# Cross-attention and a routed feed-forward part: x comes transposed from memory, its mean is spread by TensorE, and the first batch runs its softmax by halves

## The chip, the cores and the metric

One core of a Trainium2 chip. The metric is device microseconds (us) of one execution. The profiled execution has times of its own, from the hardware profiler.

## The reference

Eight batches (b) of 224 queries and 750 context rows, width 2048, all float32. A layer norm of x, attention of the normalised rows on the context (which is key and value), a residual, a second layer norm, and then a dense layer with sixteen low-rank experts, the top two per row.

```python
def xattn(query, key):
    a = jnp.einsum('bqd,bkd->bqk', query, key)
    e = jax.nn.softmax(a, axis=-1)
    return jnp.einsum('bqk,bkd->bqd', e, key)

x = x + xattn(layernorm(x), ctx)
n = layernorm(x)
base = n @ base_w.T + base_b
hidden, logits = n @ A.T, n @ router_w.T
combine = top-2 of softmax(logits), renormalised
out = x + base + 0.5 * sum over e of combine[e] * (hidden @ B[e].T)
```

## The kernel before

Every product is made of three matmuls of a faster type: an operand is split into a high part (ScalarE copies it into that type) and a low part (VectorE subtracts the high part from the operand), and TensorE adds high x high, high x low and low x high. So in front of each product stands a chain of two engines.

**Batches.** `one(b, stage)` exists on each engine: once for batch 0 ("first"), in a loop for batches 1 to 6 ("mid"), and once for batch 7 ("last"); then come the dense layer and the experts, GT = 56 tiles, which the change leaves as they are. Within a batch TensorE goes through:

- *Scores* (`scores_of`, L753 to L755): the width is 16 blocks k of 128, taken as 8 pairs j. For each pair and each half q of the queries (112 rows each) 2 x 6 matmuls. The context comes transposed from memory (`ctxT`), with four slots in SBUF, but only HR = 2 slots for its high part. So pair j goes ScalarE `ctx_high` (L995, waits until TensorE has done pair j - 2), VectorE `ctx_low` (L1216), TensorE. Each engine has an order written by hand, in which other work is put between the pairs.
- *The batch before* rides along: VectorE takes the statistics of its result x2 (`stats`, L1230), aggregates (L1234), GpSimd raises the variance to -1/2 (L1648), VectorE makes the shift (L1243), ScalarE normalises (L1008, queued between the high parts of pairs 3, 4 and 5), TensorE transposes it (`x2T_of`, L790: 8 transposes of 112x128 a group, 4 groups, ahead of pairs 5, 6, 7 and behind the last), and makes the hidden rows and router logits (L806 to L808). GpSimd adds high and low part of the transposed rows into `xT_st` to be stored.
- *Softmax*: VectorE row maximum (L1248), ScalarE exponentials (L1022), TensorE transposes them (L833).
- *Values* (`outputs_of`, L856 to L858): 24 tiles e (four column chunks c of six row tiles t), six matmuls each. `value_high` (L1017) may run four tiles ahead (NR = 4), `value_low` (L1226) follows it. After a chunk VectorE adds the residual (`residual`, L1261).
- *The next batch's x*: `xn` is loaded (L542), VectorE takes its statistics (half of them in the softmax, half at tiles 4 and 5), ScalarE normalises it at tiles 9 and 10 (L1008), TensorE transposes it in four groups ahead of tiles 13, 14, 16 and 17 (L790), and ScalarE and VectorE split it into `nT_h` and `nT_l` (L989, L1212). x is loaded a second time, into `x2`, for the residual (L549).

The transposes pass through two PSUM slots (`work`), numbered over all stages by `JOBS`: `filled` counts those that TensorE has written, `drained` those that VectorE has read. All loads are issued by SyncE's queue in one written order (`one` under `block.sync`), each behind its waits.

## Time and profile before

| | |
|---|---|
| Median of 3 runs | 1377.2 us (1376.44 to 1383.87) |
| Profiled execution: its own time | 1379.78 us |
| Profiled execution: span from first to last instruction | 1378.0 us |
| TensorE busy | 1344.8 us, 98% |
| VectorE, ScalarE, GpSimd busy | 68%, 45%, 22% |
| Mean granted clock of TensorE | 0.995 of full speed |
| HBM traffic over the span | 261 GB/s |

Busy means that an instruction of the engine was under way; TensorE's matmuls overlap, so their start-to-start distance, not their length, is what one costs. The chain that ended last follows the work back from the end, so its rows tell which engine set the time at each moment.

### The profile page before, as it was taken

Reading aid. Unit: us, or ns where it says so; the run is one execution under the profiler, and the core shown is the slowest. Engines: PE = TensorE matmul, PEld = TensorE weight load, DVE = VectorE, ACT = ScalarE, POOL = GpSimd, SP = SyncE. Lnnn points to the kernel's source line nnn. Section 1 sums busy time; section 2 is a strip of 40 time slices with the busy share of each in tenths; the row PEclk is TensorE's granted clock in tenths of the full one; section 3 lists DMA queues with packets and bytes.
Section 4 is the critical chain, followed back from the end, with each engine's and each line's share of the span. In section 5 each row is a group of like instructions: output and inputs, shape, how many; then the busy total and the mean of one; then the engine's idle time right before and its main releaser. Section 6 shows DMA issues by size and latency. Waiting matters only on the chain.

```text
span 1378.0 us, 17969 instructions
## 1 busy us (share of the span) xinstructions
PE 1344.8 (98%) x6777; PEld 1103.3 (80%) x6777; DVE 936.5 (68%) x1193; ACT 625.3 (45%) x777; POOL 306.4 (22%) x233
## 2 busy tenths in 40 slices
PE   5999999999999999999999999999999999999998
PEld 4778888887878888787888877888788888888887
DVE  6567778778777878868557366787787664464644
ACT  3355655545555554555411356777776211111110
POOL 2001102020200202020614732444453111111110
PEclk9999999999999999999999999999999999999999
DMA  8967768787877868869666678999995978879785
GB/s 297 296 202 256 238 234 249 238 278 242 261 217 257 259 217 262 262 211 234 224 182 170 211 218 271 313 325 318 323 293 149 341 240 260 263 252 284 239 276 160
DMA packets 160248, 345.34 MB, mean 251 GB/s; under 512 B 51680, under 2 KB 68064, under 8 KB 145760
## 3 DMA queue, kind: packets, MB, share of 16 engines
q1 hardware_dynamic: 141600, 277.06, 64.9%
q0 software_dynamic: 10528, 52.85, 12.2%
q10 hardware_dynamic: 8064, 14.68, 3.0%
q8 instruction: 35, 0.57, 0.2%
q14 instruction: 21, 0.17, 0.0%
HBM read 260.87 MB, written 99.41 MB: 261 GB/s over the span
## 4 chain that ended last, share of the span: by engine, by line
PE 82%; DMA 7%; DVE 5%; POOL 3%; issue 2%; ACT 1%; SPq 0%; ACTq 0%; DVEq 0%; POOLq 0%
PE scores L887 11%; PE scores L889 11%; PE scores L888 11%; PE scores L753 6%; PE scores L755 6%; PE scores L754 6%; PE scores L856 6%; PE scores L858 6%; PE scores L857 6%; PE work L790 3%; PE work L923 2%; PE work L924 2%; DMA y_scratch<-y_out,yrow_i 2%; POOL hs_scratch L1706 2%; DMA x<-in_x_dram 2%
## 5 line engine op out<-in xcount | busy, mean ns | idle before, releaser
L887 PE MATMUL scores<-w_h,a_h 128*128 128x512 f32 x896 | 352.0, 393 | 3.3 <-DVE w_l L1464 3.3
L889 PE MATMUL scores<-w_h,a_l 128*128 128x512 f32 x896 | 351.0, 392 | 0.0
L888 PE MATMUL scores<-w_l,a_h 128*128 128x512 f32 x896 | 350.3, 391 | 0.0
L1091 ACT ACTIVATE a_h<-a_in 128x512 fp32r<-128x512 f32 x148 | 83.6, 622 | 315.2 <-DMA a_in<-xT_scratch 205.3
L887 PEld LDWEIGHTS scores<-w_h,a_h 128*128 128x128 f32 x896 | 168.3, 188 | 40.9 <-DVE w_l L1464 4.1
L889 PEld LDWEIGHTS scores<-w_h,a_l 128*128 128x128 f32 x896 | 168.3, 188 | 37.8
L888 PEld LDWEIGHTS scores<-w_l,a_h 128*128 128x128 f32 x896 | 168.4, 188 | 37.0
L1473 DVE TENSOR_TENSOR a_l<-a_in,a_h 128x512 fp32r<-128x512 f32 x148 | 107.5, 774 | 122.2 <-ACT a_h L1091 118.6
L1226 DVE TENSOR_TENSOR raw_l<-raw_in,val_h 128x512 fp32r<-128x512 f32 x192 | 155.6, 827 | 49.1 <-ACT val_h L1017 48.3
L753 PE MATMUL scores<-ctxT_h,nT_h 128*112 128x494 f32 (+1 forms) x512 | 173.4, 339 | 1.1 <-DVE nT_l L1212 1.1
L755 PE MATMUL scores<-ctxT_h,nT_l 128*112 128x494 f32 (+1 forms) x512 | 171.1, 334 | 0.0
L754 PE MATMUL scores<-ctxT_l,nT_h 128*112 128x494 f32 (+1 forms) x512 | 170.9, 334 | 0.0
L1017 ACT ACTIVATE val_h<-raw_in 128x512 fp32r<-128x512 f32 x192 | 118.9, 626 | 107.7 <-PE scores L858 107.7
L856 PE MATMUL scores<-val_h,eT_h 128*112 128x512 f32 (+1 forms) x384 | 156.9, 409 | 5.9 <-DVE raw_l L1226 4.0
L1216 DVE TENSOR_TENSOR ctxT_l<-ctxT_in,ctxT_h 128x1500 fp32r<-128x1500 f32 x64 | 109.4, 1719 | 70.4 <-ACT ctxT_h L995 69.5
L858 PE MATMUL scores<-val_h,eT_l 128*112 128x512 f32 (+1 forms) x384 | 152.9, 398 | 0.0
L857 PE MATMUL scores<-raw_l,eT_h 128*112 128x512 f32 (+1 forms) x384 | 152.6, 397 | 0.0
L995 ACT ACTIVATE ctxT_h<-ctxT_in 128x1500 fp32r<-128x1500 f32 x64 | 92.4, 1454 | 121.5 <-PE scores L755 110.5
L1531 DVE TENSOR_TENSOR b_hl<-b_in,b_hl 64x2048 fp32r<-64x2048 f32 x43 | 99.6, 2319 | 42.4 <-ACT b_hl L1107 39.4
L1673 POOL TENSOR_TENSOR res<-res,bias_b 128x512 f32<-128x512 f32 x42 | 63.6, 1516 | 290.1 <-DMA res<-x_scratch 265.9
L1648 POOL TENSOR_TENSOR rs<-ve,mhalf 112x2 f32<-112x2 f32 x16 | 15.4, 964 | 420.4 <-DVE ve L1238 420.4
L1664 POOL TENSOR_TENSOR xT_st<-nT_h,nT_l 128x896 f32<-128x896 f32 x32 | 72.4, 2267 | 157.7 <-DVE nT_l L1212 157.7
(150 smaller groups left out, 1981.9 us busy)
## 6 DMA issues: line engine op xcount, KB each, us to landing
ctxT_in<-in_ctxT_dram SPq DMA_DIRECT2D x64, 750.0 KB, 7.6
raw_in<-in_ctx_dram SPq DMA_DIRECT2D x32, 1280.0 KB
a_in<-xT_scratch SPq DMA_DIRECT2D x37, 1024.0 KB
w_in<-in_wT_dram SPq DMA_DIRECT2D x32, 512.0 KB, 10.4
x<-in_x_dram SPq DMA_DIRECT2D x8, 1792.0 KB, 10.4
y_add<-y_scratch SPq DMA_DIRECT2D x56, 256.0 KB, 7.0
late_y<-y_scratch SPq DMA_DIRECT2D x56, 256.0 KB, 6.2
xn<-in_x_dram SPq DMA_DIRECT2D x7, 1792.0 KB, 15.4
```

What stands on the lines that cost most here:

```text
L753: pe.matmul(out, qh, ch, start=(k == 0), stop=False)
L754: pe.matmul(out, qh, cl, start=False, stop=False)
L755: last = pe.matmul(out, ql, ch, start=False, stop=(k == KD - 1))
L856: pe.matmul(out, eh, vh, start=(t == 0), stop=False)
L857: pe.matmul(out, eh, vl, start=False, stop=False)
L858: last = pe.matmul(out, el, vh, start=False, stop=(t == NT - 1))
L887: pe.matmul(o, ah, wh, start=(k == 0), stop=False)
L888: pe.matmul(o, ah, wl, start=False, stop=False)
L889: last = pe.matmul(o, al, wh, start=False, stop=(k == KD - 1))
L1017: act.activation(val_h[0:rows, e % NR, :], raw_in[0:rows, c, t, :], ACT.Copy).then_inc(val_high, 1)
L1216: dve.tensor_tensor(ctxT_l[:, j % LR, :, :], ctxT_in[:, j % LR, :, :], as_f32(ctxT_h[j % HR][:, :, :]), ALU.subtract).then_inc(ctx_ready, 1)
L1226: dve.tensor_tensor(raw[0:rows, c, t, :], raw_in[0:rows, c, t, :], as_f32(val_h[0:rows, e % NR, :]), ALU.subtract).then_inc(val_ready, 1)
```

## The change

x is handed over in a second layout, `xT`: for each batch 128 partitions x 16 blocks x 224 queries. The kernel loads that in place of transposing, into `xT_in`, which lies on the same bytes as `nT_l`. The rows of x are then loaded once per batch, into one of two buffers in turn (`rows`), and serve for the statistics and for the residual. Of the layer norm only the mean is taken off ahead of the scores: TensorE transposes a broadcast of the mean (`spread_mean`, ahead of tile 10), which gives a row of means on all partitions, and VectorE subtracts it in four parts (`centre`, at tiles 14 and 17 and at pairs 2 and 4 of the next batch). The factor 1/sigma goes into the exponentials, as their scale, and into the row maximum, by one more small multiplication. High and low parts of x stand at tiles 16, 17, 19, 20 and at pairs 3 and 5. VectorE's statistics of the next x stand at tiles 4 to 7, those of the old batch at pairs 0 and 2 (five and three), and the shift is moved behind pair 3's `ctx_low`. The next load of rows stands where the second load of x stood; in batch 7 the first four weights are loaded there too, later than before.

Batch 0 still normalises and transposes its own rows; for its residual x is loaded again. It takes pairs 6 and 7 together, first for half 0 of the queries and then for half 1, with the transposes of half 0's exponentials between the two pairs of half 1, and the first four value tiles for half 0, then for half 1. The loops over batches 1 to 6 are written out.

```diff
-LN1_AT = (9, 10)
-QT_AT = (13, 14, 16, 17)
+STATS_AT = (4, 5, 6, 7)
+MEAN_AT = 8
+SPREAD_AT = 10
+CENTRE_AT = (14, 17)
+X_HIGH_AT = (16, 19)
+X_LOW_AT = (17, 20)
...
-            nT_l = sb("nT_l", [P, KD, LQ], F32R, first)
+            nT_l, xT_in = sb_in("nT", [P, KD, LQ], first)
...
+        rows = [xn, x2]
+        mean_b = bias_b[:, 0, 0:LQ]
...
+            def load_row(b):
+                sp.dma_start(rows[b % 2][:, :, :], x_v[b]).then_inc(row_loaded[b % 2], 16)
+            def load_xT(b):
+                sp.dma_start(xT_in[:, :, :], xT[b]).then_inc(xT_loaded, 16)
...
                 if not last:
                     if first:
+                        load_row(1)
                         sp.wait_ge(filled, job_no("pre", 0, "qT", NX - 1) + 1)
-                    else:
-                        sp.wait_ge(filled, job_no("mid", b, "x2T", 0))
-                    sp.dma_start(xn[:, :, :], x_v[b + 1]).then_inc(xn_loaded, 16)
+                        sp.dma_start(xn[:, :, :], x_v[0]).then_inc(xres_loaded, 16)
                     for j in range(LR - 1):
                         score_done(sp, b, NPC - LR + j)
                         load_ctxT(b + 1, j)
                 if not first:
                     sp.wait_ge(filled, job_no(stage, b, "x2T", NX - 1) + 1)
-                sp.dma_start(x2[:, :, :], x_v[b]).then_inc(xres_loaded, 16)
                 if not last:
+                    if not first:
+                        load_row(b + 1)
                     score_done(sp, b, NPC - 1)
                     load_ctxT(b + 1, LR - 1)
+                    if not first:
+                        sp.wait_ge(filled, job_no(stage, b, "hid") + 1)
+                        sp.wait_ge(xT_staged, b * NX)
+                    load_xT(b + 1)
                     raw_again(b, 0)
...
+                if stage == "first":
+                    pe.wait_ge(ctx_ready, b * NPC + NPC)
+                    pe.wait_ge(drained, job_no("pre", 0, "qT", NX - 1) + 1)
+                    for q in range(NQ):
+                        for k in range(KD - 2 * CP, KD - CP):
+                            last = products(k, q)
+                        if q == NQ - 1:
+                            last.then_inc(score_step, 1)
+                            exps_T(stage, b, 0)
+                        for k in range(KD - CP, KD):
+                            last = products(k, q)
+                        last.then_inc(scores_done, 1)
+                    return
...
+            def spread_mean(stage, b):
+                pe.wait_ge(aggr1, (b + 2) * NQ)
+                for q in range(NQ):
+                    take(job_no(stage, b, "mB", q))
+                    pe.transpose(place(stage, "mB", q)[:, 0:QT], mv1[:, q, 0:1].to_broadcast([QT, P]),
+                                 ident[0:QT, 0:QT]).then_inc(filled, 1)
...
+                if stage == "first":
+                    pe.wait_ge(drained, job_no(stage, b, "eT", 0) + 1)
+                    for e in range(NR):
+                        if e == NR - 1:
+                            exps_T(stage, b, 1)
+                        pe.wait_ge(val_ready, b * (CH * NT) + e + 1)
+                        value_products(b, e, 0)
                 pe.wait_ge(drained, job_no(stage, b, "eT", NQ - 1) + 1)
+                if stage == "first":
+                    for e in range(NR):
+                        value_products(b, e, 1).then_inc(val_used, 1)
...
-                    if stage != "last" and e in QT_AT:
-                        pe.wait_ge(ln1_done, b * NQ + NQ)
-                        transpose_rows(stage, b, "qT", xn, QT_AT.index(e))
+                    if stage != "last" and e == SPREAD_AT:
+                        spread_mean(stage, b)
...
-            with pe.Fori(1, NB - 1) as b:
+            for b in range(1, NB - 1):
...
+            def x_high_part(b, n):
+                act.wait_ge(centred, (b - 1) * NX + n + 1)
+                act.activation(four_blocks(nT_h, n), four_blocks(xT_in, n), ACT.Copy).then_inc(x_high, 1)
             def one(b, stage):
                 for j in range(HR, NPC):
                     ctx_high(b, j)
+                    if stage != "first" and j in (3, 5):
+                        x_high_part(b, 2 + (j - 3) // 2)
...
+            def centre(b, n):
+                if n == 0:
+                    dve.wait_ge(xT_loaded, b * 16)
+                    dve.wait_ge(filled, job_no(stage_of(b - 1), b - 1, "mB", NQ - 1) + 1)
+                    dve.tensor_copy(mean_b.rearrange("a (q p) -> a q p", q=NQ),
+                                    work[:, :, 0:QT]).then_inc(drained, NQ)
+                    dve.wait_ge(drained, job_no(stage_of(b - 1), b - 1, "mB", NQ - 1) + 1)
+                cut = slice(4 * n, 4 * n + 4)
+                dve.tensor_tensor(xT_in[:, cut, :], xT_in[:, cut, :],
+                                  mean_b.unsqueeze(1).to_broadcast([P, 4, LQ]), ALU.subtract).then_inc(centred, 1)
...
+                dve.reduce_max(nraw[:, q:q + 1], all_scores(q), AX.X, negate=True).then_inc(max_step, 1)
+                dve.wait_ge(rstd1, b + 1)
+                dve.wait_ge(max_step, (b - 1) * NQ + q + 1)
+                dve.tensor_tensor(nmax[:, q:q + 1], nraw[:, q:q + 1], rs1[:, q:q + 1],
+                                  ALU.mult).then_inc(max_ready, 1)
...
                 for j in range(NPC):
+                    if j >= HR:
+                        ctx_low(b, j)
                     if old and j == 3:
                         shift(mv2, rs2, nb2, rstd2, bias2, b - 1)
-                    if j >= HR:
-                        ctx_low(b, j)
-                    if old and j < 2:
-                        if j == 0:
-                            dve.wait_ge(x2_done, b * (NQ * CH))
-                        for i in range(4 * j, 4 * j + 4):
-                            stats(x2, st2, stat2, i)
+                    if old and j == 0:
+                        dve.wait_ge(x2_done, b * (NQ * CH))
+                        for i in range(5):
+                            stats(rows[(b - 1) % 2], st2, stat2, i)
                     if old and j == 2:
+                        for i in (5, 6, 7):
+                            stats(rows[(b - 1) % 2], st2, stat2, i)
+                        dve.wait_ge(stat2, b * (NQ * CH))
                         aggregate(st2, mv2, aggr2)
                         variance(mv2, ve2, aggr2, var2, b - 1)
+                    if old and j in (2, 4):
+                        centre(b, 2 + (j - 2) // 2)
+                    if old and j in (3, 5):
+                        x_low_part(b, 2 + (j - 3) // 2)
...
+                    if new and e in STATS_AT:
+                        n = STATS_AT.index(e)
+                        if n == 0:
+                            dve.wait_ge(row_loaded[(b + 1) % 2], (b + 2) // 2 * 16)
+                        for i in range(2 * n, 2 * n + 2):
+                            stats(rows[(b + 1) % 2], st1, stat1, i)
```

## Rows read from the trace of the kernel before

**Rows 1.** The page, section 1: busy us of each engine and share.
```profile
PE 1344.8 (98%) x6777; PEld 1103.3 (80%) x6777; DVE 936.5 (68%) x1193; ACT 625.3 (45%) x777; POOL 306.4 (22%) x233
```

**Rows 2.** The chain that ended last, by time: start us, us, what.
```profile
50.08 24.61 DMA x<-in_x_dram
...
163.34 0.77 PE work L790 x8
...
242.62 0.77 PE work L790 x8
...
725.42 1.11 DVE hg L1289
```

**Rows 3.** Timeline of TensorE, values of batches 1 and 2.
```profile
163.18 0.93 PE L790 MATMUL work<-ident,xn 112*128 112x112 f32 x8
163.88 0.47 PE L856 MATMUL scores<-val_h,eT_h 128*112 128x512 f32 x1
...
226.96 0.30 PE L822 MATMUL work<-ident,hT 80*112 80x80 f32 x2
```

**Rows 4.** The page, section 6: DMA issues, KB, us to landing.
```profile
x<-in_x_dram SPq DMA_DIRECT2D x8, 1792.0 KB, 10.4
```

**Rows 5.** Timeline of TensorE, scores of batch 2.
```profile
181.55 0.39 PE L753 MATMUL scores<-ctxT_h,nT_h 128*112 128x494 f32 x1
...
189.69 0.28 PE L755 MATMUL scores<-ctxT_h,nT_l 128*112 128x256 f32 x1
189.94 0.47 PE L753 MATMUL scores<-ctxT_h,nT_h 128*112 128x494 f32 x1
```

**Rows 6.** Timeline of VectorE, start of batch 2.
```profile
183.19 4.85 DVE L1230 BATCH_NORM_STATS2 st<-x 112x6 f32<-112x512 f32 x8
188.16 1.72 DVE L1216 TENSOR_TENSOR ctxT_l<-ctxT_in,ctxT_h 128x1500 fp32r<-128x1500 f32 x1
189.80 0.38 DVE L1234 BATCH_NORM_AGGREGATE mv<-st 112x2 f32<-112x24 f32 x2
```

**Rows 7.** Timeline of ScalarE, start of batch 2.
```profile
185.97 1.46 ACT L995 ACTIVATE ctxT_h<-ctxT_in 128x1500 fp32r<-128x1500 f32 x1 [6.46 <-PE scores L755]
...
191.38 2.10 ACT L1008 ACTIVATE x<-x,nb,rs 112x2048 f32<-112x2048 f32 x1
```

**Rows 8.** Groups by shape: busy us, mean ns.
```profile
L1212 DVE TENSOR_TENSOR nT_l<-work,nT_h 128x896 fp32r<-128x896 f32 x64 | 69.4, 1086 | 15.3 <-ACT nT_h L989 15.2
```

**Rows 9.** Timeline of GpSimd: the power operation beside VectorE.
```profile
68.80 1.66 POOL L1648 TENSOR_TENSOR rs<-ve,mhalf 112x2 f32<-112x2 f32 x1 [49.55 <-DVE ve L1238]
...
190.46 0.69 POOL L1648 TENSOR_TENSOR rs<-ve,mhalf 112x2 f32<-112x2 f32 x1 [36.81 <-DVE ve L1238]
...
231.82 1.10 POOL L1648 TENSOR_TENSOR rs<-ve,mhalf 112x2 f32<-112x2 f32 x1 [9.58 <-DVE ve L1238]
```

**Rows 10.** Timeline of VectorE, beside the last of these.
```profile
231.67 1.29 DVE L1226 TENSOR_TENSOR raw_l<-raw_in,val_h 128x512 fp32r<-128x512 f32 x2
```

**Rows 11.** Timeline of TensorE: its idle times, in square brackets.
```profile
55.86 0.79 PE L833 MATMUL work<-ident,prob 112*128 112x112 f32 x6 [1.27 <-ACT prob L1022]
58.37 0.49 PE L856 MATMUL scores<-val_h,eT_h 128*112 128x512 f32 x1 [1.71 <-DVE eT_l L1212]
...
76.78 0.77 PE L856 MATMUL scores<-val_h,eT_h 128*112 128x512 f32 x1 [2.68 <-DVE raw_l L1226]
...
994.37 0.50 PE L923 MATMUL work<-b_hl,s_hh 128*128 128x512 f32 x1 [1.19 <-DVE y_out L1539]
```

**Rows 12.** Stretches: busy us by engine, granted clock, DMA share, GB/s.
```profile
70.00:75.00 5.00, 4.10 (x18) 2.79 (x16) 1.13 (x4) 4.31 (x3) 0.46 (x1) 1.00 0.99 301
76.00:84.00 8.00, 7.22 (x20) 5.23 (x21) 4.29 (x8) 2.11 (x4) 0.00 (x0) 0.57 0.27 78
994.00:999.00 5.00, 4.63 (x20) 3.85 (x21) 3.48 (x4) 3.36 (x4) 3.25 (x2) 1.00 0.77 276
```

**Rows 13.** Timeline of VectorE, batch 0, the low part of pair 7.
```profile
47.08 1.72 DVE L1216 TENSOR_TENSOR ctxT_l<-ctxT_in,ctxT_h 128x1500 fp32r<-128x1500 f32 x1 [1.20 <-ACT ctxT_h L995]
```

More of the change, by code:

```diff
@@ L162, in xattn_ffn_kernel @@
         "pre": group("qT", NX),
-        "first": group("eT", NQ) + group("qT", NX),
-        "mid": BEFORE + group("eT", NQ) + OLD + group("qT", NX),
+        "first": group("eT", NQ) + group("mB", NQ),
+        "mid": BEFORE + group("eT", NQ) + OLD + group("mB", NQ),
         "last": BEFORE + group("eT", NQ) + OLD,
@@ L189, in act_no, with side_of, stage_of @@
         return number(stage, b, (name, n), BY_ACT)
+    def side_of(b, c):
+        return (c + 1) % 2 if b > 0 else c % 2
+    def stage_of(b):
+        return "first" if b == 0 else "mid"
     def slot_of(stage, name, n=0):
@@ L756, in products @@
                     return last
-                for j in range(NPC - 1):
+                for j in range(NPC - 1 if stage != "first" else NPC - 2):
                     if stage != "first" and j in X2T_BEFORE:
-                        x2T_of(stage, b, b - 1, x2, (X2T_BEFORE.index(j),))
+                        x2T_of(stage, b, b - 1, rows[(b - 1) % 2], (X2T_BEFORE.index(j),))
                     if stage == "first" and j in (1, 2):
@@ L837, in outputs_of, with exps_T @@
-            def outputs_of(stage, b):
+            def exps_T(stage, b, q):
+                pe.wait_ge(exp_done, b * NQ + q + 1)
+                take(job_no(stage, b, "eT", q))
+                slot = slot_of(stage, "eT", q)
+                for t in range(NT):
+                    at = (t // 3) * BANK + (t % 3) * QT
+                    last = pe.transpose(work[:, slot, at:at + QT],
+                                        prob[:, q, t * P:(t + 1) * P], ident[0:QT, 0:QT])
+                last.then_inc(filled, 1)
@@ L863, in one @@
                 if stage != "first":
-                    x2T_of(stage, b, b - 1, x2, (NX - 1,))
+                    x2T_of(stage, b, b - 1, rows[(b - 1) % 2], (NX - 1,))
                     hidden_of(stage, b, 0, HID_EARLY)
-                exps_T(stage, b)
+                if stage != "first":
+                    for q in range(NQ):
+                        exps_T(stage, b, q)
                 if stage != "first":
@@ L1047, in one @@
                     high(stage, b, "x2T", NX - 1, four_blocks(nT_h, NX - 1), 2, 2 * LQ)
+                three = lambda q: eT_h[:, q, :, :].rearrange("p (k i) c -> p k (i c)", k=2)
+                if stage == "first":
+                    high(stage, b, "eT", 0, three(0), 2, 3 * QT)
                 exponentials(b, 1)
-                for q in range(NQ):
-                    high(stage, b, "eT", q, eT_h[:, q, :, :].rearrange("p (k i) c -> p k (i c)", k=2), 2, 3 * QT)
+                for q in range(1 if stage == "first" else 0, NQ):
+                    high(stage, b, "eT", q, three(q), 2, 3 * QT)
                 for e in range(NR, CH * NT):
@@ L1121, in _ @@
             one(0, "first")
-            with act.Fori(1, NB - 1) as b:
+            for b in range(1, NB - 1):
                 one(b, "mid")
@@ L1410, in one, with exps_low @@
                         value_low(b, 2 * (j - (NPC - 2)) + 1)
+                def exps_low(q):
+                    three = lambda tile: tile[:, q, :, :].rearrange("p (k i) c -> p k (i c)", k=2)
+                    low(stage, b, "eT", q, three(eT_h), three(eT_l), 2, 3 * QT)
                 row_max(b, 0)
@@ L1416, in one @@
                     x2T_low(NX - 1)
-                if new and old:
-                    dve.wait_ge(xn_loaded, b * 16 + 16)
-                    for i in range(4):
-                        stats(xn, st1, stat1, i)
-                for q in range(NQ):
-                    three = lambda tile: tile[:, q, :, :].rearrange("p (k i) c -> p k (i c)", k=2)
-                    low(stage, b, "eT", q, three(eT_h), three(eT_l), 2, 3 * QT)
+                for q in range(0 if old else 1, NQ):
+                    exps_low(q)
                 if old:
@@ L1446, in one @@
                         tile_low(0, (FIRST_A_AT.index(e),))
-                    if new and e - 3 in QT_AT:
-                        n = QT_AT.index(e - 3)
-                        low(stage, b, "qT", n, four_blocks(nT_h, n), four_blocks(nT_l, n), 2, 2 * LQ)
                     if c >= 1 and t == 3:
@@ L1562, in _ @@
             one(0, "first")
-            with dve.Fori(1, NB - 1) as b:
+            for b in range(1, NB - 1):
                 one(b, "mid")
```

133 lines of the change are left out of this document (68 added, 65 removed).

## The prediction

> **What bounds the kernel now.** I read the page first: TensorE is busy for 98% of the span, VectorE 68%, ScalarE 45% [rows 1]. Then the chain in order of time. It returns to the same transposes every 79.28 us (163.34 to 242.62) and names almost nothing but TensorE between batch 1 and batch 6, so in the attention part a microsecond taken off TensorE is a microsecond of the program, as long as nobody makes it wait. Batch 0 is the exception: the chain there has a DMA of 24.61 us, the second load of x [rows 2]. The routed part behind batch 7 is not touched; I carry it over whole. Last I laid the timelines of TensorE, VectorE and ScalarE side by side for batch 2, where the change puts new work.
>
> The sum is made against the profiled execution: span 1378.0 us, its own time 1379.78 us. The median of the runs is 1377.2, so 2.6 below that execution; I carry every difference over to the median. A difference under 0.5% (6.9 us) can't be told from none by a measurement of this kernel.
>
> **Transposes of x out of the value stage.** One group of eight starts at 163.18 and the next value product at 163.88; the chain gives the group 0.77 us [rows 2, 3], restart included. Four groups in each of batches 0 to 6: 28 x 0.77 = -21.6 us. Added are two transposes of the mean per batch. The pair of the hidden part takes 0.30 with its tail [rows 3]; the new ones are as wide as those of x (0.77/8 = 0.10 each), so 2 x 0.10 and about 0.07 of restart = 0.26, times 7 = +1.8 us. ScalarE loses the two normalisations per batch; it is off the path there, worth nothing.
>
> **VectorE in the value stage.** Per batch the eight statistics now all stand at value tiles 4 to 7 (four stood in the softmax before), and a copy of the mean, two subtractions of it and two low parts stand at 14 to 20. A value tile is 6 x 0.231 = 1.39 us on TensorE. Tiles 4 to 10 ask VectorE for 7 low parts of 0.61, 8 statistics of 0.6, 0.8 for mean and variance, 0.45 for the hidden copy and 1.6 for the first residual: 11.9 us against 9.7 of TensorE, with about 2.3 us of lead at the start. It just fits, with 0.3 us left at tile 10. Tiles 14 to 21 ask 12.3 against 11.1, with about 3 of lead: fits. I take 0. The bound is the row load: it is issued where the load of x was, behind the last transposes of the old batch, and that one took 10.4 us to land [rows 4]; tile 4's statistics come 9 us after the issue (the hidden transposes ahead of tile 2 are at 226.96 [rows 3]). A load that is 1.4 late eats the lead and costs 0.9 per batch, 5.4 us. Against it: the load of xn that stood ahead of it in the queue is gone, 1.8 MB less backlog. The transposed x is issued at the start of the values and is wanted 16 us later: hidden.
>
> **VectorE and ScalarE in the score stage: the new wait.** Here the order of the hand-offs is what counts. A pair of context blocks j needs TensorE's j-2 done, then ScalarE's high part (1.46), then VectorE's low part (1.72), and TensorE spends 4.13 on a pair ((189.81-181.55)/2 [rows 5]). That leaves 0.6 us of slack a pair. Batch 2 by the new order: five statistics from 183.19 at 0.6 end at 186.2; the high part of pair 2 ends at 185.97+1.46 = 187.43; its low part starts there (before, it stood behind eight statistics until 188.16 and ended at 189.88, and TensorE, free at 189.81, began at 189.94 with a restart of 0.08: 0.2 gained) [rows 5, 6, 7]. Then VectorE issues at 189.10 three statistics (1.8), aggregation (0.4), variance (0.1) and the subtraction of the mean. The latter has no row; the low part of the same 896 elements takes 1.09 [rows 8], an operation of that size with a broadcast operand 1.11 [rows 2]. I take 1.05, bounds 0.5 and 1.6. So pair 3's low part starts at 192.6 and ends at 194.3; TensorE wants it at 189.81+4.13 = 193.9: it stops for 0.4, and 0.08 of restart. The shift, which before ran ahead of that low part, is now behind it: 194.2+0.16 = 194.4. ScalarE's first normalisation of the old batch waits for the shift, holds ScalarE for 2.0 and is queued ahead of the high part of pair 4: 196.4 + 1.46 = 197.9, low part to 199.6. TensorE wants pair 4 at 194.4+4.13 = 198.5: it stops for 1.1 and 0.08 more. Pair 5 has the old batch's transposes ahead of it and is on time. Net of the 0.2 gained: +1.5 us in each of batches 1 to 7, +10.5 us. Bounds: with the subtraction at 0.5 it is +0.9 a batch, at 1.6 it is +2.5; and a reason to be all wrong would be that the old order has slack I don't see, 0.
>
> The small power operation on GpSimd stands between variance and shift. It takes 0.69 when VectorE is idle and 1.10 when two low parts run beside it, once 1.66 [rows 9]; the low parts beside the 1.10 still took 1.29 for two, their usual 0.61 apiece and a tail [rows 10]. So I take it done by 193.2, before the shift is due, at no cost; if it is held until pair 3's low part is through (as the 1.66 was), the shift moves 0.7 back, +4.9 us over seven batches. The Trainium skill's page "SBUF — State Buffer", section "SBUF: two separate sides", says that a VectorE operation with two SBUF inputs and a GpSimd operation that reads SBUF exclude each other for a whole instruction, the loser fully blocked. By that rule GpSimd's 0.69 would also be added to pair 3's low part, +0.7 a batch, or about 5 us in all; the row of 1.29 for two low parts beside it doesn't show it.
>
> The extra product of the row maximum with 1/sigma (0.2 us, twice) delays the exponentials; the transposes that wait for them had about 1.4 us to spare. And the low parts of the exponentials lose the four statistics ahead of them, 0.1 gained. I take -0.1 a batch, -0.6 us.
>
> **Batch 0.** Before: softmax and the second load of x leave TensorE idle for 1.27, 1.71 and 2.68 us [rows 11], and after the last the clock is at its lower level for a while: 0.57 of full speed from 76 to 84 [rows 12], 0.43 x 8 = 3.4 us, some 0.5 of it on idle time, so 2.9 lost. The batch ends a period before 181.55, at 102.3. In the new queue the load of x stands right behind the row of batch 1 and no longer behind three contexts; the 2.68 and its clock are gone. What comes instead: TensorE now waits for pairs 6 and 7 before it starts pair 6. It would start at 45.6 (the high part of pair 7 waits for the same event, 47.08-1.46), but pair 7's low part ends at 48.80 [rows 13]: 3.2 us idle, and the clock falls after such a gap [rows 11, 12], 2 more. The halves then hide most of the softmax (0.5 is left); the exponentials of the second half leave 1.1; and the four tiles done by halves take VectorE's lead away in front of its statistics (2). Last, the transposed x of batch 1: x and all ahead of it landed at 50.08+24.61 = 74.7 with a full queue [rows 2, 12]; behind it come 0.75 and 1.8 MB at 301 GB/s, so it lands near 83. VectorE asks for it at tile 14, from about 80, and then owes the copy, two subtractions, a low part, the residual and the low parts of tiles 15 to 18, 7.6 us in all: tile 18 starts at 90.6, and six tiles of 1.39 end at 98.9. That is 3.4 us ahead, of which 3.1-0.3 = 2.8 are the transposes and the mean already counted: -0.6 beside the terms above. Bounds: 0 to 8 us ahead.
>
> **Loops written out, instructions fetched once each.** Batches 0 and 7 are written out already, under a full DMA queue, and TensorE's waits there have data behind them. 0. Weights 0 to 3 load 16 us later in batch 7 and are wanted at tile 15: hidden. HBM traffic is the same.
>
> **Sum.** -21.6 +1.8 +10.5 -0.6 -0.6 = -10.5. Median 1377.2-10.5 = 1366.7 us (0.8% faster), a mid batch 77.9 instead of 79.3. Its own range, with batch 0 and the subtraction at their nearer values, 1361 to 1371.
>
> **Rivals.**
> 1. The score stage has no new wait. For it: only 0.4 and 1.1 us. Against: each hand-off has its row. 1366.7-10.5 = 1356.
> 2. The score wait is a step bigger, by GpSimd's late power operation or a row load that lands late: +5, so 1371.6, within 0.5%. For it: 1.66 in one row; 10.4 us of landing.
> 3. Slower: the score-stage wait lets the clock fall in every batch. The place is pair 4; the price by the row of batch 0 is 2.9 us, seven times 20.3, so 1387. It decides where a gap grows past the 1.19 at 994 (full clock after it) toward 2.68 (clock fell) [rows 11, 12]. My gap is 1.1, with 0.4 four microseconds ahead of it.
> 4. Nothing changes: VectorE, with 4 us more work a batch, gives the 3 us back in the values as well. 1376.
>
> **Chances.** Forecast 0.48, rival 1 0.14, rival 2 0.20, rival 3 0.08, rival 4 0.10. Faster by over 0.5%: most of the forecast (0.42), rival 1, a fourth of rival 2: 0.61. Slower: 0.08. Same: 0.31. Range: from rival 1 to rival 4, 1355 to 1377.
>
> **What would show it.** The transposes of x fall from 512 to 288 and the mean's 14 appear. TensorE's idle time ahead of the first score product of pairs 3 and 4, released by the low part of the context, is 0.4 and 1.1 us in batches 1 to 7 (10 us in all, 1.1 before). ScalarE's normalisation starts near 12.9 us after the batch's first score, not 9.8. In batch 0 a gap of 3 us ends at 48.9 and no wait for x. I am wrong if the period of a mid batch is 76.3 (rival 1) or 79 (rival 4), if the granted clock falls in mid batches (rival 3), or if batch 0 ends later than 102.

## The result and the profile after

The changed kernel takes 1375.0 us (median of 14 runs, 1372.1 to 1376.7); the kernel before, timed beside it, 1381.0 us (14 runs, 1373.6 to 1386.2). The ratio is 0.9959, 95% interval 0.9942 to 0.9976: 0.41% or 6 us faster, under the 0.5% that the prediction set as its bound, and 8 us over its 1366.7. The profiled execution has a span of 1373.0 us.

The page's first section after the change (busy us, share of the span, instructions), beside [rows 1]:

```profile
PE 1330.2 (97%) x6567; PEld 1083.7 (79%) x6567; DVE 968.8 (71%) x1235; ACT 599.2 (44%) x763; POOL 325.4 (24%) x233
```

VectorE has 32 us more to do, TensorE 15 us less. I laid the start of every batch and stage of both timelines beside each other (us). A batch and its score stage begin with the first score product; the value stage goes from the first value product to the next batch:

| | before | after | forecast of the difference |
|---|---|---|---|
| start of batch 1 | 102.23 | 98.69 | -3.4, measured -3.5 |
| score stage, batches 1 to 7 | 42.3 to 42.6 | 44.6 | +1.4, measured +2.05 |
| value stage, batches 1 to 6 | 36.74 | 33.85; batches 3, 5, 6: 34.56, 34.04, 34.35 | -2.8, measured -2.9 and +0.2 for late rows, on average |
| start of batch 7 | 578.16 | 570.68 | -11.9, measured -7.5 |
| from there to the end | 799.9 | 802.3 | +1.4, measured +2.5 |

The chain of the changed kernel in batch 2 (start, us, what; of the 15 longest pieces between 60 and 240 us these are the batch's) shows where the score stage loses its time:

```profile
181.44 1.47 ACT ctxT_h L1061
182.93 1.72 DVE ctxT_l L1286
184.65 1.80 DVE st L1301 x3
187.14 3.10 POOL rs L1749
190.63 1.84 issue
192.47 1.44 ACT ctxT_h L1061
193.93 1.73 DVE ctxT_l L1286
```

[Rows 2] had almost nothing but TensorE here. Now the chain leaves it for GpSimd's power operation `rs`: 3.10 us, where [rows 9] have 0.69. The same place on the timeline of VectorE:

```profile
186.89 0.17 DVE L1309 TENSOR_SCALAR ve<-mv 112x2 f32<-112x2 f32 x1
186.97 1.09 DVE L1338 TENSOR_TENSOR nT_in<-nT_in,bias_b 128x896 f32<-128x896 f32 x1
187.97 1.71 DVE L1286 TENSOR_TENSOR ctxT_l<-ctxT_in,ctxT_h 128x1500 fp32r<-128x1500 f32 x1
190.26 0.16 DVE L1314 SCALAR_TENSOR_TENSOR nb<-mv,rs 112x2 f32<-112x2 f32 x1 [0.58 <-POOL rs L1749]
```

`ve` frees GpSimd at 187.06. VectorE goes straight on with the subtraction and pair 3's low part, until 189.68. The power operation is under way all that time and ends 0.55 us behind them, and the shift `nb` comes at 190.26. Behind it on ScalarE, in its order:

```profile
190.46 2.10 ACT L1074 ACTIVATE x<-x,nb,rs 112x2048 f32<-112x2048 f32 x1 [1.42 <-DVE nb L1314]
192.47 1.43 ACT L1061 ACTIVATE ctxT_h<-ctxT_in 128x1500 fp32r<-128x1500 f32 x1
```

The old batch's normalisation, then pair 4's high part; VectorE's low part follows at 193.93, and TensorE, which was through with pair 3 at 194.1, waits:

```profile
195.71 0.48 PE L779 MATMUL scores<-ctxT_h,nT_h 128*112 128x494 f32 x1 [1.61 <-DVE ctxT_l L1286]
```

That gap is 1.61 or 1.62 us in each of batches 1 to 7. It does not bring the clock down. The windows behind the gap and over the mid batches (PEclk is the third number from the end):

```profile
195.00:203.00 8.00, 7.29 (x46) 6.35 (x47) 5.76 (x5) 6.89 (x8) 0.00 (x0) 1.00 0.98 339
100.00:660.00 560.00, 546.47 (x3056) 445.92 (x3055) 469.32 (x605) 291.55 (x352) 96.30 (x43) 1.00 0.78 243
```

In batch 0 the forecast gap is there, at its length (3.2 forecast), with a granted clock of 0.60 from 51 to 55 us behind it, and so is the gap of the second half's exponentials:

```profile
50.89 0.75 PE L779 MATMUL scores<-ctxT_h,nT_h 128*112 128x494 f32 x1 [3.30 <-DVE ctxT_l L1286]
...
66.20 0.49 PE L893 MATMUL scores<-val_h,eT_h 128*112 128x512 f32 x1 [1.01 <-DVE eT_l L1282]
```

### The profile page after: what moved, and what is told of

Same layout as the page of the kernel before. It is cut to its first block, busy times and chain, and to the rows that moved or that the text cites. A ratio compares the mean times of both kernels' runs of the same rounds, so it can differ in the third digit from the quotient of the medians.

```text
span 1373.0 us, 16807 instructions
## 1 busy us (share of the span) xinstructions
PE 1330.2 (97%) x6567; PEld 1083.7 (79%) x6567; DVE 968.8 (71%) x1235; ACT 599.2 (44%) x763; POOL 325.4 (24%) x233
## 4 chain that ended last, share of the span: by engine, by line
PE 79%; DVE 5%; DMA 4%; issue 2%; ACT 2%; POOL 1%; ACTq 0%; DVEq 0%; POOLq 0%
PE scores L953 14%; PE scores L955 14%; PE scores L954 14%; PE scores L893 6%; PE scores L895 6%; PE scores L894 6%; PE scores L779 4%; PE scores L781 4%; PE scores L780 4%; DMA y_scratch<-y_out,yrow_i 2%; PE work L989 2%; PE work L990 2%; PE work L840 2%; DVE ctxT_l L1286 2%; ACT ctxT_h L1061 1%
## 5 line engine op out<-in xcount | busy, mean ns | idle before, releaser
L779 PE MATMUL scores<-ctxT_h,nT_h 128*112 128x494 f32 (+1 forms) x512 | 175.8, 343 | 16.2 <-DVE ctxT_l L1286 14.6
L1574 DVE TENSOR_TENSOR a_l<-a_in,a_h 128x512 fp32r<-128x512 f32 x148 | 103.9, 749 | 105.6 <-ACT a_h L1161 101.7
L893 PE MATMUL scores<-val_h,eT_h 128*112 128x512 f32 (+1 forms) x384 | 153.9, 401 | 3.2 <-DVE raw_l L1296 1.4
L1749 POOL TENSOR_TENSOR rs<-ve,mhalf 112x2 f32<-112x2 f32 x16 | 31.5, 1966 | 403.3 <-DVE ve L1309 403.3
L779 PEld LDWEIGHTS scores<-ctxT_h,nT_h 128*112 128x112 f32 x512 | 90.6, 177 | 33.2 <-DVE ctxT_l L1286 18.4
```

Of the source, the lines that this page charges most:

```text
L779: pe.matmul(out, qh, ch, start=(k == 0), stop=False)
L893: pe.matmul(out, eh, vh, start=(t == 0), stop=False)
```

## The experiments

Fourteen runs follow; two of them (e9, e12) are the two kernels unchanged. A time without an interval is one execution, and of such times only the stages are compared: the part from the first score of batch 7 to the end, whose code differs only in that batch, takes between 794.8 and 802.3 us in these profiles.

### What holds the score stage: e1, e2, e6

e1 takes the subtraction out from between variance and low part:

```diff
-                    if old and j in (2, 4):
-                        centre(b, 2 + (j - 2) // 2)
+                    if old and j == 4:
+                        centre(b, 3)
...
+                    if new and e == 22:
+                        centre(b + 1, 2)
```

> The third subtraction of the mean (part 2) is moved from VectorE's pair 2 to value tile 22 of the batch before; all else as in the changed kernel. In the changed kernel pair 3 of a mid batch starts 12.62 us after the batch's first score and pair 4 at 18.60, TensorE idle 1.61 ahead of it, and the power operation on GpSimd lasts 3.10. Theory A (GpSimd is shut out while VectorE's operations with two SBUF inputs follow each other without a break): the power operation lasts 2.0 to 2.4 since only the low part of pair 3 stands beside it, pair 3 at 12.4, pair 4 at 17.7, so 0.9 off a batch and 6 us in all. Theory B (the power operation is slow for another reason, the wait is only the sum of VectorE's own work): it stays at 3.1, and pair 4 moves by less than 0.3 since the shift still waits for it. Theory C (the port costs nothing): 0.7 to 1.1 for the power operation, pair 4 at 17.0.

Measured: 1364.8 us. Pair 4 starts 17.70 after the first score, the score stage is 43.69, 0.9 less in every batch. GpSimd and VectorE in batch 2:

```profile
186.93 2.19 POOL L1751 TENSOR_TENSOR rs<-ve,mhalf 112x2 f32<-112x2 f32 x1 [31.28 <-DVE ve L1309]
```

```profile
186.85 1.72 DVE L1286 TENSOR_TENSOR ctxT_l<-ctxT_in,ctxT_h 128x1500 fp32r<-128x1500 f32 x1
```

The low part ends at 188.57, the power at 189.12: again 0.55 behind. Theory A, to the digit.

e2 leaves the subtraction and puts the shift ahead of the low part:

```diff
+                    if old and j == 3:
+                        shift(mv2, rs2, nb2, rstd2, bias2, b - 1)
                     if j >= HR:
                         ctx_low(b, j)
-                    if old and j == 3:
-                        shift(mv2, rs2, nb2, rstd2, bias2, b - 1)
```

> One part undone: the shift of the old batch stands ahead of pair 3's low part again, all else as in the changed kernel. VectorE then has to wait for GpSimd behind the subtraction of the mean. Theory A: the power operation lasts about 2.1 (shut out during the one subtraction, then 0.7 alone), the shift comes near 11.7 us after the batch's first score, pair 3 starts at 13.5, pair 4 at 17.7 with no idle time ahead of it: 0.9 off a batch. The rival, that the order of shift and low part is worth nothing because it only moves the wait from pair 4 to pair 3: pair 4 stays at 18.3 to 18.6.

Measured: 1363.7 us. Pair 3 at 13.36, pair 4 at 17.57, the score stage 43.46:

```profile
184.48 1.46 POOL L1749 TENSOR_TENSOR rs<-ve,mhalf 112x2 f32<-112x2 f32 x1 [31.25 <-DVE ve L1309]
```

```profile
184.31 1.09 DVE L1338 TENSOR_TENSOR nT_in<-nT_in,bias_b 128x896 f32<-128x896 f32 x1
185.97 0.16 DVE L1314 SCALAR_TENSOR_TENSOR nb<-mv,rs 112x2 f32<-112x2 f32 x1 [0.58 <-POOL rs L1749]
186.05 1.72 DVE L1286 TENSOR_TENSOR ctxT_l<-ctxT_in,ctxT_h 128x1500 fp32r<-128x1500 f32 x1
```

VectorE now stops behind the subtraction, and GpSimd gets in there: the power ends 0.54 behind the subtraction's end at 185.40. Both pairs come as theory A has them, 0.1 earlier still; only the power is shorter than its 2.1. The rival (pair 4 at 18.3 to 18.6) is out.

e6 puts an operation with one input in the power's place:

```diff
-                pool.tensor_tensor(rs[:, :], ve[:, :], mhalf[:, :], ALU.pow).then_inc(sem_rstd, 1)
+                pool.tensor_scalar(rs[:, :], ve[:, :], 1.0, None, ALU.add).then_inc(sem_rstd, 1)
```

> The changed kernel, but GpSimd's power of two inputs (variance and exponent) is an addition of a constant to one input, so 1/sigma is replaced by a wrong value and the output is not the reference's; every order and wait is the same. It asks whether GpSimd is shut out beside VectorE's subtractions because it reads two inputs, or because it reads and writes SBUF at all. Theory A (any GpSimd operation on SBUF is shut out until VectorE's run of two-input operations has ended): the operation lasts 2.9 to 3.1 us in the score stage of every batch as the power does (3.09), pair 4's first score stands 18.6 us after the batch's first. Rival B (one input gets through): it lasts under 1 us, VectorE's shift starts right behind pair 3's low part without the 0.58 of idle time, and pair 4 starts at 18.0 to 18.1, 3.5 us less over seven batches. Rival C: in between, it ends during the low part but the start is delayed by the subtraction.

Measured: 1366.3 us, score stage 44.1, pair 4 at 18.12. GpSimd, and the low part beside it:

```profile
187.72 2.61 POOL L1749 TENSOR_SCALAR rs<-ve 112x2 f32<-112x2 f32 x1 [32.06 <-DVE ve L1309]
```

```profile
188.55 1.71 DVE L1286 TENSOR_TENSOR ctxT_l<-ctxT_in,ctxT_h 128x1500 fp32r<-128x1500 f32 x1
```

It is shut out as well, until VectorE's run ends at 190.26, and is through 0.07 later. So A for the blocking; pair 4 stands where B had it, because an addition needs 0.5 us less than the power once it is let in. What the profile gives as the power's length is two things: waiting for VectorE's run to end, and 0.55 behind it.

### Batch 0: e3, e4

e3 runs batch 0 in the old order (pairs 6 and 7 apart, softmax and values whole).

> The halves of batch 0 undone: scores, softmax and values of batch 0 in the order of the kernel before; transposed x, mean and everything else as in the changed kernel. Theory A (the halves cost more by the double wait at pair 6 and by the lost lead of VectorE at tiles 4 to 10 than they hide of the softmax; it is the earlier load of x that helps): batch 1 starts at 95 to 96.5 instead of 98.7. Rival (the halves are what shortens batch 0): batch 1 starts later than 99, since the softmax leaves 3 us idle again and the clock falls behind it.

Measured: 1368.7 us. TensorE's gaps are the two of before [rows 11]:

```profile
58.33 0.79 PE L870 MATMUL work<-ident,prob 112*128 112x112 f32 x6 [1.27 <-ACT prob L1065]
60.84 0.49 PE L881 MATMUL scores<-val_h,eT_h 128*112 128x512 f32 x1 [1.71 <-DVE eT_l L1257]
```

Batch 0 takes 76.8 us, 2.7 less than in the changed kernel, and batch 1 starts at 96.1: theory A. The first pair of batch 0 takes 4.9 to 7.7 us in these traces, whatever the kernel, so it is better left out: from the second pair on, batch 0 takes 69.7 here and 72.7 in the changed kernel (72.7 in e1, e2 and e6 too, whose batch 0 is the same; 74.0 in e12, where the lower clock lasts longer). So the halves with their double wait cost 3.0 us more than they hide. e4 keeps the halves and splits their wait:

```diff
-                    pe.wait_ge(ctx_ready, b * NPC + NPC)
+                    pe.wait_ge(ctx_ready, b * NPC + NPC - 1)
...
+                        if q == 0:
+                            pe.wait_ge(ctx_ready, b * NPC + NPC)
```

> As the changed kernel, but in batch 0 TensorE waits for the context of pair 6 before pair 6 and for that of pair 7 only before the first product of pair 7. Theory A (the double wait costs its 3.3 us and the clock behind it): the idle time ahead of pair 6 is gone, 1.3 is left in front of pair 7's first product, the clock stays up and the values of batch 0 begin 3 to 4 us earlier (61.5 now), batch 1 starts near 95. Rival (another wait takes its place, VectorE's statistics or the transposed x, which lands at 79.7): batch 1 starts less than 1 us earlier.

Measured: 1371.0 us, batch 0 takes 76.2, 3.3 less, and its values begin at 57.9 instead of 61.5: theory A. What is left of the gap, now ahead of pair 7, left the clock up (the product takes 0.48, not 0.75, and the granted clock is 1.00 from 46 to 60 us):

```profile
50.82 0.48 PE L779 MATMUL scores<-ctxT_h,nT_h 128*112 128x494 f32 x1 [1.26 <-DVE ctxT_l L1288]
...
62.58 0.48 PE L895 MATMUL scores<-val_h,eT_h 128*112 128x512 f32 x1 [1.01 <-DVE eT_l L1284]
```

From the second pair on it takes 69.6 us, no less than the 69.7 of e3 without any halves. So the 3.0 us are the double wait; the halves by themselves bring nothing that one profile of each shows.

### The orders together: e7, e8

e7 is e1, e2 and e4 in one kernel.

> The changed kernel with three orders of the first four experiments together: the shift stands ahead of pair 3's low part, the subtraction for part 2 of x is moved from the score stage to value tile 22 of the batch before, and in batch 0 TensorE waits for pair 6 first and for pair 7 only after it. Theory A (what the change lost is the VectorE queue between variance and shift, and the single wait in batch 0): variance is followed by nothing, the power takes 0.69 to 0.75 us beside an idle VectorE, pair 3 starts 12.6 to 12.8 us and pair 4 16.8 to 17.0 us after the batch's first score with no gap over 0.3, the score stage takes 42.6 to 42.8 (44.59 in the changed kernel, 42.55 before), seven times -1.9 = -13, batch 0 is 3.3 shorter: 16 us under the changed kernel, about 1359 us, 1.6% under the kernel before. Rival B: the subtraction at value tile 22 is in the way of the next batch's first low parts and gives 0.5 to 1 us a batch back: 1362 to 1366. Rival C: the idle 0.7 us on VectorE only moves the gap to pair 3: it starts at 13.3 and the score stage stays at 43.4, about 1364.

Measured: 1357.7 us (6 runs), ratio to before 0.9834, 0.9800 to 0.9868. Pair 3 at 12.59, pair 4 at 16.79, score stage 42.68 in batches 2 to 7, where the kernel before has 42.6 (42.3 in batch 7). Batch 1 takes 43.14, and batch 0 is 2.6 shorter from its second pair on, not 3.3. GpSimd has VectorE out of its way:

```profile
183.83 0.69 POOL L1753 TENSOR_TENSOR rs<-ve,mhalf 112x2 f32<-112x2 f32 x1 [31.28 <-DVE ve L1311]
```

Theory A; what the changed kernel lost in these stages is the place of three steps. Batch 3's value stage is still 34.47 and batch 5's 34.48. e8 moves the statistics for that:

```diff
-STATS_AT = (4, 5, 6, 7)
-MEAN_AT = 8
-SPREAD_AT = 10
+STATS_AT = (6, 7, 8, 9)
+MEAN_AT = 10
+SPREAD_AT = 12
```

> e7 and in addition the statistics of the new batch at value tiles 6 to 9 instead of 4 to 7 (mean and variance at 10, spread of the mean by transposes at 12). Theory A (in batch 3, and at times in batches 1, 5 and 6, VectorE waits at tile 4 for a row load of 10 us): the wait at the statistics is gone, batch 3's value stage falls from 34.8 to 33.85 and all seven are alike, 1 to 2 us less than e7. Rival B: the statistics then collide with the first residual at tile 9 and the lead is gone at tile 10: every value stage is 0.5 us or more longer, 3 us or more slower than e7. Rival C: no difference: the late load of batch 3 is only the last of several waits there.

Measured: 1359.1 us (6 runs), 0.9841, 0.9809 to 0.9872, not to be told from e7. The value stages of batches 1 to 6 are 34.43 to 34.45: the wait is gone, and batches 1 to 6 pay 0.6 for it each, as rival B had it, though not with its 3 us in the whole.

### The written-out loops: e5, e9 to e14

e5 is the kernel before with this edit on TensorE, ScalarE and VectorE:

```diff
-            with pe.Fori(1, NB - 1) as b:
+            for b in range(1, NB - 1):
```

> The kernel before with nothing changed but its three loops over batches 1 to 6 written out, as the change writes them. Theory A (the forecast: instructions fetched once each cost nothing under a full DMA queue): the same time as the kernel before within 0.2%, score stage of a mid batch (first score to first value) 42.6 us and its period 79.3, as before; the instruction queue's packets rise from 35 to about 50. Rival B: part of the small result is the price of the written-out loops: 3 to 6 us slower than the kernel before, with gaps on TensorE that nothing releases. Rival C: a loop turn costs something at its branch, so writing it out alone gains 1 us or more over six batches.

Measured: 1372.2 us (10 runs; before 1382.3), ratio 0.9934, 0.9909 to 0.9959. Theories A and B missed. C's number is met by the mid batches, which gain 0.16 us each (79.17), 1 us in all, but the kernel is faster by more than the whole change. In the two profiles the rest lies where there is no loop: 5.0 us behind the first score of batch 7 and 2.3 us in batch 0, where the second load of x takes 22.7 us in place of 24.6, and the gap of 3.31 ahead of the product that waits for `w_l` (841.14 in the kernel before) is not there.

> The kernel before, unchanged, profiled a second time. In its first profile TensorE had gaps of 2.68 us at 76.78 and 3.31 us at 841.14 that the profile of the same kernel with its loops written out (e5, 0.66% faster) lacks, while its mid batches differ by only 0.16 us each. Theory A (the loops cause the gaps in some lasting way): both gaps are there again, each over 2 us, and the period of a mid batch is 79.3. Theory B (a load in batch 0 and one in the routed part land earlier or later from one execution to the next): at least one of the two is gone or under 1 us, and others may stand elsewhere; the period is 79.3 all the same.

Measured: 1378.8 us; period 79.3, batch 0's gap 1.80 in place of 2.68, so that neither theory is met in full (both gaps are there, one of them under 2 us), and:

```profile
838.80 0.80 PE L887 MATMUL scores<-w_h,a_h 128*128 128x512 f32 x1 [3.32 <-DVE w_l L1464]
```

> The kernel before with TensorE's loop over batches 1 to 6 written out and the loops of ScalarE and VectorE kept. Theory A (what e5 gained comes from TensorE's own loop, its registers and the code behind it): nearly all of e5's gain, 7 to 9 us under the kernel before. Theory B (it comes from ScalarE and VectorE, whose hand-offs are late in loops): under 2 us, and the period of a mid batch stays at 79.3. Theory C (both, or neither but the amount of code): half of it, 3 to 6 us.

Measured: 1373.7 us, 0.9957, 0.9933 to 0.9982; no gap near 838, x in 22.7.

> The kernel before with the loops of ScalarE and VectorE written out and TensorE's kept. Theory A: under 2 us. Theory B: nearly all of e5's gain of 9 us, and the 0.16 us of a mid batch (pair 2 at 8.31 us behind the first score, not 8.39). Theory C: 3 to 6 us, and e10 and e11 together make e5.

Measured: 1379.0 us, 1.000, 0.9977 to 1.0024; period 79.2; the gap is there, x takes 24.7:

```profile
836.58 0.50 PE L887 MATMUL scores<-w_h,a_h 128*128 128x512 f32 x1 [3.06 <-DVE w_l L1464]
```

So it is TensorE's loop, theory A of these two, if at 6 us by the ratio a little short of its range. In these traces each fetch of TensorE's instructions brings 16 KB (queue q8). One stood 19 to 20.5 us behind the first issue of `w_in` for the dense layer (at 801.66 in the kernel before) where the gap was, 16 to 16.6 us where it was not. e13 and e14 move the fetches, with nothing but waits that are already fulfilled (e13's edit; e14 has 401 of them, on e5's kernel).

```diff
-            pe.wait_ge(ident_ready, 2)
+            for _n in range(129):
+                pe.wait_ge(ident_ready, 2)
```

> The kernel before, loops and all, with 64 more instructions at the start of TensorE's program: 128 waits, two to an instruction, for a semaphore that has already been reached, in the 14 us in which TensorE waits for x anyway. They do nothing but push all that stands behind them 64 instructions further along TensorE's fetches, each of which brings 16 KB (0.57 MB in 35). Theory A (TensorE's gap of 3.3 us near 838, in all three profiles with TensorE's loop kept and in none with it written out, comes when a fetch falls 18 to 21 us after the first load of w_in is issued, as in those three; with the loop written out it falls 16 us after): the fetch falls 13 to 15 us after that issue, the third w_h starts 23 us after it instead of 26, and the gap is gone; time 2 to 5 us under the kernel before. Theory B (the loop itself, not the place of the fetch, causes it): the gap of 3 us is there, and the time is that of the kernel before within 2 us.

Measured: 1378.0 us, 0.9985, 0.9956 to 1.0014. The fetch moved, to 15.8 us behind the issue; the gap stayed, a little shorter:

```profile
840.47 0.50 PE L887 MATMUL scores<-w_h,a_h 128*128 128x512 f32 x1 [2.50 <-DVE w_l L1465]
```

> The kernel of e5 (before, loops written out) with 200 more instructions of that kind at the start of TensorE's program, which move the fetch that fell 41 us after the first issue of w_in to about 20 us after it. Theory A: the gap of 3 us before the weights' product, absent in e5, appears near 835, and the time rises by 2 to 4 us over e5 (1372.2; the start may be late by some us too, to be read apart at the first score). Theory B: no gap, the routed part as in e5.

Measured: 1385.7 us, 1.0028, 1.0001 to 1.0054, of which 8.3 are a late start (first score at 27.36, e5 19.02). The fetch stands 20 us behind the issue, and with the loop written out the gap is back:

```profile
841.73 0.50 PE L887 MATMUL scores<-w_h,a_h 128*128 128x512 f32 x1 [2.16 <-DVE w_l L1465]
```

e13 contradicts the theory of the fetch, e14 that of the loop. What decides on this gap stays open; in batch 0 x took 23.8 to 25.0 us in the four traces with TensorE's loop and 22.3 to 22.7 in the three without, which no run explains.

> The changed kernel, unchanged, profiled a second time and timed beside e10 and e11. All theories expect the score stage of 44.59 us and the value stage of 33.85 again, with batch 3's at 34.3 to 34.9. Theory A (the rest of what the routed part does is the state of its transfers in each execution): its gap of 2.62 us at 986.66 is 0.7 to 2.7 us long, as in the experiments so far, and the span from batch 7's first score to the end is 797 to 802 us (802.3 in the first profile, 799.8 before). Theory B (the part behind batch 7 is slower in the changed kernel for good): 802 again, within 0.5 us. Time 1375, ratio 0.995 to 0.997.

Measured: 1374.1 us (10 runs), 0.9962, 0.9940 to 0.9984. Score stage 44.58, value stage 33.85 and batch 3's 34.55, batch 5's 35.08. The part behind batch 7's first score takes 798.4, as theory A has it; the late gap is 0.35, under its 0.7.

## Why the prediction was wrong

**The stages moved the way that was forecast, the total did not follow**: -6 for -10.5. The transposes are gone from the values, and the new wait is at pair 4 of the scores; the size of that wait is the term that failed. That the total came out faster at all is in part luck, since an edit that the sum had at 0, the loops, is worth as much by itself (below). The total also lies beside rival 4's 1376, but what rival 4 says did not happen.

**The step that failed** is in the score stage: "So I take it done by 193.2, before the shift is due, at no cost", said of the power operation. It was done when pair 3's low part was, plus 0.55, and pair 4 came 0.5 us later than worked out. The stage grew by 2.05 a batch for +1.4 with the softmax (+1.5 without), over 4 us in the program. That is rival 2, nearly at its price of 4.9. The row that gave the answer was among those I weighed: the 1.66 at 68.80 [rows 9] ends at 70.46, 0.55 behind the two low parts beside it, and the shift comes then. VectorE's timeline of the kernel before:

```profile
68.62 1.29 DVE L1226 TENSOR_TENSOR raw_l<-raw_in,val_h 128x512 fp32r<-128x512 f32 x2
70.50 0.16 DVE L1243 SCALAR_TENSOR_TENSOR nb<-mv,rs 112x2 f32<-112x2 f32 x1 [0.59 <-POOL rs L1648]
```

I took the other pair, where the power ended after 1.10, for the rule. There it ends at 232.93, 0.56 behind the first of the two low parts, and the second runs beside it at its usual length:

```profile
231.67 0.69 DVE L1226 TENSOR_TENSOR raw_l<-raw_in,val_h 128x512 fp32r<-128x512 f32 x1
232.28 0.68 DVE L1226 TENSOR_TENSOR raw_l<-raw_in,val_h 128x512 fp32r<-128x512 f32 x1
```

So in the kernel before the power got in between two operations of VectorE in the value stages of batches 1 to 6, but not in batch 0, and in none of the seven score stages of the changed kernel. What decides this no run shows.

The Trainium skill's page "SBUF — State Buffer", section "SBUF: two separate sides", says that the loser is fully blocked; in e1, e2 and e6 the trace agrees for GpSimd. The second low part beside the 1.10 is at odds with it, since neither of the two was held up there. For its other direction, VectorE shut out by GpSimd, the prediction had +0.7 a batch. At the power operation it doesn't show: VectorE was there first, and the low part takes 1.71 or 1.72 in all of them. It does show later in the same stage, in both kernels, where GpSimd's addition for `xT_st` gets in behind the first of two low parts. The two then take 3.23 us instead of 1.29, and end 0.56 behind GpSimd's:

```profile
204.48 2.45 POOL L1765 TENSOR_TENSOR xT_st<-nT_h,nT_l 128x896 f32<-128x896 f32 x1 [14.25 <-DVE nT_l L1282]
```

```profile
204.26 3.23 DVE L1296 TENSOR_TENSOR raw_l<-raw_in,val_h 128x512 fp32r<-128x512 f32 x2
```

**Pair 3's stop** was 0.24 (12.62 after the first score; 12.38 in e1, where nothing is late), 0.4 forecast; the subtraction took 1.09, 1.05 taken. Its bound of +2.5 a batch for a subtraction of 1.6 adds up to +2.0 by the prediction's own path. **Transposes out, mean in**: the value stage is 2.9 shorter, 2.8 forecast.

**Softmax.** The extra product of the row maximum, taken at 0.2 twice, takes 0.16 for the first half and, in six of seven batches, 1.27 for the second, beside another addition for `xT_st` that began first:

```profile
215.44 2.12 POOL L1765 TENSOR_TENSOR xT_st<-nT_h,nT_l 128x896 f32<-128x896 f32 x1 [2.75 <-DVE nT_l L1282]
```

```profile
216.31 1.27 DVE L1326 TENSOR_TENSOR nmax<-nraw,rs 112x1 f32<-112x1 f32 x1
```

No wait of TensorE comes of it.

**Late rows.** "I take 0" for VectorE held at the tiles, but not for the load. In batch 3 VectorE waits for the row issued at 293.98:

```profile
304.31 1.29 DVE L1301 BATCH_NORM_STATS2 st<-xn 112x6 f32<-112x512 f32 x2 [1.23 <-DMA xn<-in_x_dram]
```

The value stages of batches 3, 5 and 6 are 0.7, 0.2 and 0.5 us longer than the others, 1.4 in all; the prediction had this as 0.9 a batch or nothing. e8 shows that starting later is no cure.

**Batch 0** came out near the forecast -3.4 in the first profile, by other terms. No wait for the transposed x: it was issued at 62.06, landed 17.6 us later, at 79.7, where I had 83, and VectorE asked for it at 82.0, with the copy of the mean:

```profile
62.06 0.88 SPq L542 DMA_DIRECT2D nT_in<-in_xT_dram  x1
```

```profile
82.01 0.38 DVE L1334 COPY bias_b<-work 128x224 f32<-128x224 f32 x1
82.43 1.09 DVE L1338 TENSOR_TENSOR nT_in<-nT_in,bias_b 128x896 f32<-128x896 f32 x1
```

From the second pair on, batch 0 of the changed kernel is 5.6 us shorter than before's in the first two profiles and 0.8 in the second two (e9, e12), so the agreement has little weight. That the double wait is a loss, and that the halves without it bring nothing visible, is shown by e3 and e4. The prediction also counted the lower clock behind the 2.68 alone. Behind the 1.27 and 1.71 of the softmax it falls as well, in the kernel before (the third number from the end):

```profile
58.00:64.00 6.00, 5.63 (x18) 4.13 (x19) 2.87 (x6) 1.26 (x2) 0.00 (x0) 0.72 1.05 315
```

**"Loops written out ... 0."** A mid batch gains 0.16 from them, 1 us in all. By e5 the written-out kernel before is as fast as the changed one (1372.2 beside 1375.0 and 1374.1; the intervals of the ratios, 0.9909 to 0.9959 and 0.9942 to 0.9976, overlap): the change's other parts, as ordered, bring nothing that was measured, and e7 shows that they are worth 14.6 us (1372.2 to 1357.7) once ordered otherwise. The changed kernel with its loops kept was not run, so how much of e5's gain is in its time is not shown.

**The rivals.** 1 (no new wait): wrong. 3 (clock falls in every batch): wrong, full clock behind a gap of 1.61. 4 (VectorE gives it back in the values): wrong, 33.85 there. The median of the kernel before was 1377.2 in three runs and 1381.0 in fourteen; by the ratio the changed kernel misses 1366.7 by 5 to 8 us either way.

## What to carry to other kernels

A small operation on GpSimd between two of VectorE can cost all that VectorE has queued behind the first: let VectorE wait for it right there, or put nothing big in between, and follow who stands behind the result. When a change moves many steps into an engine's queue, its order can be worth nearly as much as the work that it removes: here three moves were worth 17 us by the medians, where the forecast has -19.8 for the transposes and the mean. And time the mechanical part of a change (loops written out) by itself before crediting the rest.

## What the runs showed of the hardware

- GpSimd's power operation of 112x2 took 0.69 us alone, 1.46 beside one VectorE subtraction, 2.19 beside a low part, 3.09 beside both; each of these three ended 0.54 or 0.55 us behind VectorE's run. The one-input addition (2.61) ended 0.07 behind it. VectorE's own 1.09 and 1.71 did not change. In the value stages of batches 1 to 6 of the kernel before it took 1.10 and ended 0.56 behind the first of two low parts, ahead of the second's end.
- The other way round, VectorE's second low part began beside GpSimd's addition of 128x896 and ended 0.55 us behind it: 2.61 instead of 0.69, twice in each of batches 1 to 7, in both kernels.
- A gap of 1.61 us on TensorE left the granted clock at 1.00; the one of 3.30 in batch 0 was followed by products of 0.75 in place of 0.48, at 0.60 from 51 to 55 us. The length of one gap alone does not tell: behind the 1.27 and 1.71 of batch 0's softmax, with 0.8 us of work between them, the clock was 0.72 from 58 to 64 us in the kernel before, and fell so in six of the seven other traces that have this pair; behind the 2.16 of e14 it was 0.79 for 8.3 us, behind the 2.50 of e13 it stayed at 1.00.
- With two hundred instructions more ahead of TensorE's program a gap of 2.16 us came back some 800 us later, and TensorE's loop alone is worth 0.43% (interval 0.18 to 0.67): at this level a comparison of two kernels can also measure where their instructions lie.
